# Depthwise convolution and channel rotation: the convolution's bands made by GpSimd from a mask and taps, without loading or turning them

## The chip, the cores and the metric

The kernel runs on one core of a Trainium2 chip. Its time is device microseconds; three runs of the kernel before took 558.16, 558.51 and 558.95 us (median 558.51). One more execution was recorded by the profiler.

## The reference

`x` is 16 x 128 x 64 x 64 in f32 (image, channel, row, column). What is computed:

```python
# _gn: 32 groups of 4 channels, mean and variance over (4 channels, 64, 64) of one image
x = x + depthwise_conv5x5(_gn(x), kernel)      # one 5x5 kernel for each channel, 16 of its 25 places filled, padding 2
x = x + einsum('hvc,bchw->bvhw', R, _gn(x))    # for each row h a 128x128 matrix over channels
```

The 16 places hold taps 1 to 8 of the channel's 3x3 weight, eight with a plus and eight with a minus sign. `R` is an input of 64 x 128 x 128.

## The kernel before

**First stage**, 32 groups of four channels. A group's `x` lies in a tile of `xin` (7 tiles): partition = image half n (0, 1) times 64 rows, free = 8 images x 4 channels x 64 columns. The convolution is a sum over five column offsets d: a band matrix of 64 x 64 over the rows (made of one column of taps) times the normalised tile shifted by d. Four such 64 x 64 products (two channels, two image halves) run in the four quarters of PE; two channels are one *pair* (`convolve(k, pair)`, L423), 40 matmuls in the trace, each pair in two banks of PSUM.

The steps are software pipelined by `for s in STEPS`, s from -3 to 34, in the same order on every engine. In step s:
- VectorE (DVE): the scale and shift of round s + 1 (`affine`, L373, L375), the add `x + conv` of group s - 1's second pair (L365), the statistics of that sum (L382), the statistics of `x` of group s + 3 (L389), three small operations for `spread` of round s + 2 (L398 to L403), the add of group s's first pair.
- TensorE (PE): the variance matmul of round s + 1 (L444, waits for `spread`), the first pair of group s, the mean matmul of round s + 2 (L454), the second pair.
- ScalarE (ACT): the square root (L314), evictions of PSUM to `y` (L305), `turn_taps` of group s + 1 (L294), two of eight images normalised into `padded` (L322), evictions.
- GpSimd (POOL): six of the eight images normalised (L267), after `affine` of that group.
- SyncE (SP): issues all DMAs: x of group s + 5 (L165, eight of 128 KB, 256 bytes a packet), the tap windows of group s + 2 (L172), the sum of group s - 1 to DRAM (L179, two of 512 KB).

The bands come through DRAM: DVE writes each channel's taps into a line of 400 numbers (L358), the lines are stored, and L172 reads for each of 64 partitions a window that starts one number later, 330 KB a group. Read like this the band is mirrored, so `turn_taps` copies it backwards, in two halves. A round's second half of `affine` holds the scales of the second normalisation; they are stored every eight groups (L186) and read back in another layout (L239).

**Second stage**, 32 *granules* of four rows and eight images, 1 MB each. `load_granule` (L223) reads into one of six tiles `tin`, ScalarE normalises five images (L335) and GpSimd three (L279), PE multiplies by the turned rotation (L482, rotations turned by L468, evicted by L343), DVE adds (L414), `store_granule` (L231) writes. The tiles of both stages share one area.

## Time and profile before

| what | us |
|---|---|
| median of three runs | 558.51 |
| the profiled execution, its own time | 558.65 |
| its span, first to last instruction | 556.8 |
| busy: PE, ScalarE, DVE, GpSimd | 450.6, 361.4, 347.2, 186.0 |
| PE convolution matmuls (L434), 2560 | 297.8 |
| granted TensorE clock, mean | 0.961 |

Read it as two stages, one up to about 370 us and one from there; shares over the whole span mix both. The times of an engine's queue (SPq) are the times in which it issues a DMA, not in which the DMA runs. A matmul's recorded length overlaps that of its neighbours, since four run at once.

### The profile page before, as it was taken

To read this page: it belongs to the slowest core of one execution; us is meant where nothing else is said; L and a number is where in the kernel's file an instruction comes from. 1 tells how busy PE (TensorE), PEld (TensorE's weight loads), DVE (VectorE), ACT (ScalarE), POOL (GpSimd) and SP (SyncE) were. 2 spreads that over 40 slices of the span, in tenths; PEclk is the share of its full clock that TensorE was granted. 3 is DMA by queue.
4 is the path that set the end of the run, shared out by engine and by line. 5 is a ranking of instruction groups with operands and counts; after the bars stand their busy time and mean duration, and the time that the engine had idled before them with its cause. 6 is when DMAs were issued, how large, how long until landed. Compare 5 with 4: busy or idle time off the path is not lost.

```text
span 556.8 us, 8400 instructions
## 1 busy us (share of the span) xinstructions
PE 450.6 (81%) x3024; PEld 172.8 (31%) x3024; DVE 347.2 (62%) x649; ACT 361.4 (65%) x598; POOL 186.0 (33%) x299
## 2 busy tenths in 40 slices
PE   0169999999898898989899899962998778788772
PEld 0123333333333333333333233321443333333330
DVE  3426787877876876686778768561574544544533
ACT  1066887787777678768877888842675455455550
POOL 0223534433533533353344335301343233233230
PEclk9999999999999999899899999995899998998997
DMA  6898788989889888889988989937999999999999
GB/s 155 200 201 167 204 218 222 244 220 226 244 216 226 225 225 216 219 216 235 223 224 243 226 224 308 274 85 235 375 394 397 394 396 397 396 398 396 395 394 325
DMA packets 214329, 150.03 MB, mean 269 GB/s; under 512 B 138384, under 2 KB 179472, under 8 KB 214288
## 3 DMA queue, kind: packets, MB, share of 16 engines
q1 hardware_dynamic: 214288, 149.49, 92.0%
q8 instruction: 24, 0.39, 0.3%
q14 instruction: 17, 0.14, 0.1%
HBM read 82.14 MB, written 67.33 MB: 268 GB/s over the span
## 4 chain that ended last, share of the span: by engine, by line
SPq 30%; DMA 28%; DVE 13%; ACT 12%; PE 11%; issue 4%; DVEq 0%
SPq L165 23%; DMA out_dram<-area 21%; ACT area L305 8%; PE ps L434 7%; DMA area<-tap_lines 7%; DVE stats L382 3%; DVE area L365 3%; DVE area L414 3%; DVE stats L389 3%; SPq L179 2%; PE ps L482 2%; ACT area L294 2%; SPq L227 2%; ACT area L322 2%; SPq L172 1%
## 5 line engine op out<-in xcount | busy, mean ns | idle before, releaser
L434 PE MATMUL ps<-area 64*64 64x512 f32 x2560 | 297.8, 607 | 8.5 <-ACT area L322 8.5
L267 POOL TENSOR_SCALAR area<-area,affine 128x256 f32<-128x256 f32 x192 | 132.9, 707 | 222.1 <-DVE affine L375 222.1
L305 ACT ACTIVATE area<-ps 64x512 f32<-64x512 f32 x256 | 150.4, 587 | 10.6 <-PE ps L434 5.9
L482 PE MATMUL ps<-area 128*128 128x512 f32 x256 | 123.7, 630 | 34.9 <-ACT area L343 28.1
L434 PEld LDWEIGHTS ps<-area 64*64 64x64 f32 x2560 | 93.2, 134 | 158.5 <-issue 156.9
L414 DVE TENSOR_TENSOR area<-ps,area 128x512 f32<-128x512 f32 x128 | 81.2, 685 | 85.7 <-DMA out_dram<-area 68.6
L335 ACT ACTIVATE area<-area,norm 128x256 f32<-128x256 f32 x160 | 82.1, 588 | 72.2 <-DMA area<-x_scratch 58.5
L365 DVE TENSOR_TENSOR area<-area 128x1024 f32<-128x1024 f32 x64 | 78.8, 1232 | 77.1 <-ACT area L305 77.0
L294 ACT ACTIVATE area<-area 64x1280 f32<-64x1280 f32 x64 | 81.3, 1270 | 60.1 <-DMA area<-tap_lines 59.2
L279 POOL TENSOR_SCALAR area<-area,norm 128x256 f32<-128x256 f32 x96 | 52.0, 555 | 132.9 <-DMA area<-x_scratch 81.0
L389 DVE BATCH_NORM_STATS2 stats<-area 128x6 f32<-128x512 f32 x128 | 79.9, 685 | 10.8 <-DMA area<-in_x_dram 10.8
L382 DVE BATCH_NORM_STATS2 stats<-area 128x6 f32<-128x512 f32 x128 | 80.7, 693 | 1.1
L482 PEld LDWEIGHTS ps<-area 128*128 128x128 f32 x256 | 48.7, 199 | 99.4 <-issue 40.5
L444 PE MATMUL ps<-spread,half_mean 128*128 128x16 f32 (+1 forms) x72 | 15.0, 283 | 36.3 <-DVE spread L403 35.6
L322 ACT ACTIVATE area<-area,affine 128x256 f32<-128x256 f32 x64 | 35.0, 594 | 0.8
L314 ACT ACTIVATE std<-ps,eps 128x16 f32<-128x16 f32 (+1 forms) x36 | 9.8, 271 | 36.7 <-PE ps L444 36.0
L444 PEld LDWEIGHTS ps<-spread,half_mean 128*128 128x128 f32 x72 | 11.5, 201 | 64.5 <-DVE spread L403 60.4
L454 PE MATMUL ps<-stats,half_mean 128*128 128x16 f32 (+1 forms) x72 | 14.7, 279 | 15.1 <-DVE stats L389 12.4
L454 PEld LDWEIGHTS ps<-stats,half_mean 128*128 128x128 f32 x72 | 11.3, 198 | 41.2 <-issue 41.2
L373 DVE RECIPROCAL affine<-std 128x16 f32<-128x16 f32 (+1 forms) x36 | 8.5, 236 | 14.9 <-ACT std L314 14.9
L468 PEld LDWEIGHTS ps<-ident,rot_all 128*128 128x128 f32 x64 | 8.2, 146 | 9.2 <-issue 9.2
L468 PE MATMUL ps<-ident,rot_all 128*128 128x128 f32 x64 | 10.1, 282 | 1.0 <-DVE affine L375 1.0
(22 smaller groups left out, 38.3 us busy)
## 6 DMA issues: line engine op xcount, KB each, us to landing
area<-in_x_dram SPq DMA_DIRECT2D x256, 128.0 KB, 3.3
x_scratch<-area SPq DMA_DIRECT2D x64, 512.0 KB, 6.0
area<-x_scratch SPq DMA_DIRECT2D x32, 1024.0 KB, 12.4
out_dram<-area SPq DMA_DIRECT2D x32, 1024.0 KB, 11.3
area<-tap_lines SPq DMA_DIRECT2D x32, 330.0 KB, 5.1
tap_lines<-line SPq DMA_DIRECT2D x1, 200.0 KB, 3.1
norm_scratch<-affine SPq DMA_DIRECT2D x8, 2.0 KB
rot_all<-_L_conv_rota_matrix_dram SPq DMA_DIRECT2D x4, 0.5 KB, 10.4
```

The lines of the kernel that those rows point to most:

```text
L165: sp.dma_start(xin[slot][n * HALF:(n + 1) * HALF, :, c], x[n * J:(n + 1) * J, k * GC + c].rearrange("j h w -> h j w")).then_inc(x_landed[s ...
L267: last = nc.gpsimd.tensor_scalar(padded[k % GRING][:, :, j, PAD:PAD + W], xin[k % XRING][:, j], affine[:, k, 0, 0, j:j + 1], affine[:, k, ...
L279: last = nc.gpsimd.tensor_scalar(gn[n % NRING][:, :, j], tin[n % IRING][:, :, j], norm2[:, n % 2, 0, j:j + 1], norm2[:, n % 2, 1, j:j + 1] ...
L294: nc.scalar.activation(taps[k % 2][n * HALF:(n + 1) * HALF], taps_raw[k % 2][0:H, :, :, H - 1::-1], ACT.Identity).then_inc(taps_ready, 1)
L305: last = nc.scalar.activation(y[k % YRING][rows, 2 * pair + c], ps[half, bank + n].rearrange("p (j w) -> p j w", j=J), ACT.Identity)
L335: last = nc.scalar.activation(gn[n % NRING][:, :, j], tin[n % IRING][:, :, j], ACT.Identity, scale=norm2[:, n % 2, 0, j:j + 1], bias=norm2 ...
L365: nc.vector.tensor_tensor(part, part, xin[k % XRING][:, :, cs].rearrange("p j c w -> p c j w"), ALU.add).then_inc(x1_ready, 1)
L382: last = nc.vector.bn_stats(out=stats[:, (s + 3) % 2, 1, 2 * q:2 * q + 2].rearrange("p j f -> p (j f)"), in_=y[(s - 1) % YRING][:, :, 2 * ...
L389: last = nc.vector.bn_stats(out=stats[:, k % 2, 0, 2 * q:2 * q + 2].rearrange("p j f -> p (j f)"), in_=xin[k % XRING][:, 2 * q:2 * q + 2]. ...
L414: nc.vector.tensor_tensor(tout[n % ORING][:, :, h], ps[:, (n * RH + h) % 6, :].rearrange("p (j w) -> p j w", j=J), tin[n % IRING][:, h], A ...
L434: last = nc.tensor.matmul(ps[half, bank + n], taps[k % 2][rows, 2 * pair + c, d], padded[k % GRING][rows, 2 * pair + c, :, d:d + W], start ...
L482: nc.tensor.matmul(ps[:, m % 6, :], rot_t[u % 2][:, h], gn[n % NRING][:, h], start=True, stop=True).then_inc(rotated, 1)
```

## The change

DVE now writes the 25 places of each channel's kernel (`line` is 25 numbers wide), the rows of the kernel in backward order. They are stored twice, one copy behind the other, and loaded so that partition m of a half holds the five rows rotated by m modulo 5 (`row_taps`, [128, 5, 640]): from place b modulo 5 it reads the tap that partition m needs for output row b. A mask (1 where |m - b| <= 2) is made once. For each group GpSimd multiplies the mask (repeated for 20 channel-and-column pairs) by `row_taps` (repeated for 13 blocks of five rows): one instruction with 1300 results a partition, into one of three `taps` tiles, two groups ahead. The second input is read in steps of 640 elements. The tap windows, their loads and `turn_taps` are gone. GpSimd normalises four images and ScalarE four.

The weight's load, the loads of `row_taps` (20 in all, the first ten for the first four groups) and the norms' stores and load are issued by ScalarE. On DVE the three operations for `spread` stand ahead of the x statistics. The rotation matrices are loaded from step 24 on instead of step 26. After the last store of the first sum, SyncE issues five loads of 112 channels (groups 0 to 27), once the four waits on older stores are met, then waits for all stores, loads the other 16 channels of the five granules, and goes on with whole granules; `tin` has seven tiles.

```diff
+TRING = 3
...
-POOL_J = 6
+POOL_J = 4
...
-IRING = 6
+IRING = 7
+EARLY = 5
+EARLY_SLOTS = (4, 5, 6, 0, 1, 2, 3)
+EARLY_GROUPS = 28
...
+ROT_STEP = GROUPS - 8
...
-    tap_lines = nc.dram_tensor("tap_lines", (C, LINE), F32, kind="Internal").ap()
+    tap_rows = nc.dram_tensor("tap_rows", (2 * TAPS, C, KW), F32, kind="Internal").ap()
...
-        line = sb("line", [C, LINE])
+        line = sb("line", [C, TAPS * KW])
+        near = sb("near", [P, HALF + BAND])
+        mask = sb("mask", [P, BAND])
+        row_taps = sb("row_taps", [P, TAPS, CK])
...
+        def granule_landings(n):
+            return 16 * (n // IRING + 1) + (16 if n % IRING < EARLY else 0)
...
-            def load_taps(k):
-                window = bass.AP(tensor=tap_lines.tensor, offset=k * GC * LINE,
-                                 ap=[[1, H], [LINE, GC], [1, WINDOW]])
-                sp.dma_start(taps_raw[k % 2][0:H].rearrange("p c d h -> p c (d h)"), window
-                             ).then_inc(taps_landed[k % 2], 16)
...
-            for k in range(2):
-                load(k)
-            sp.wait_ge(line_ready, len(POS_IDX + NEG_IDX))
-            sp.dma_start(tap_lines, line[:]).then_inc(line_stored, 16)
-            load(2)
-            load(3)
-            sp.wait_ge(line_stored, 16)
-            load_taps(0)
-            load_taps(1)
-            for k in range(4, XRING - 1):
+            for k in range(XRING - 1):
                 load(k)
...
-                if group(s + 2):
-                    sp.wait_ge(taps_ready, 2 * (s + 1))
-                    load_taps(s + 2)
                 if group(s - 1):
                     sp.wait_ge(x1_ready, 2 * s)
                     store(s - 1)
...
-                if s in range(GROUPS - 6, GROUPS - 6 + ROT_LOADS):
-                    n = s - (GROUPS - 6)
+                if s in range(ROT_STEP, ROT_STEP + ROT_LOADS):
+                    n = s - ROT_STEP
                     rows = slice(n * (H // ROT_LOADS), (n + 1) * (H // ROT_LOADS))
                     sp.dma_start(rot_all[:, rows], rota_src[:, rows]).then_inc(rot_landed, 16)
...
+            def load_granule(n, channels):
                 u, half = n // 2, n % 2
...
+                return sp.dma_start(tin[n % IRING][channels].rearrange("p h j w -> p h (j w)"),
+                                    x1_dram[channels, u * RH:(u + 1) * RH, half * J:(half + 1) * J, :].rearrange(
+                                        "c h j w -> c h (j w)"))
+
+            early, late = slice(0, EARLY_GROUPS * GC), slice(EARLY_GROUPS * GC, C)
+            for k in range(YRING):
+                sp.wait_ge(x1_stored[k], 32 * (EARLY_GROUPS // YRING))
+            for n in range(EARLY):
+                sp.wait_ge(x1_ready, 2 * (XRING * ((GROUPS - 1 - EARLY_SLOTS[n]) // XRING) + EARLY_SLOTS[n] + 1))
+                load_granule(n, early).then_inc(in_landed[n], 16)
+            for k in range(YRING):
+                sp.wait_ge(x1_stored[k], 32 * (GROUPS // YRING))
+            for n in range(EARLY):
+                load_granule(n, late).then_inc(in_landed[n], 16)
...
-            load_granule(0)
-            sp.wait_ge(norm2_stored, 32 * (GROUPS // NBATCH))
-            sp.dma_start(norm2[:], norm2_dram).then_inc(norm2_landed, 16)
-            for n in range(1, IRING):
-                load_granule(n)
+            for n in range(EARLY, IRING):
+                load_granule(n, slice(0, C)).then_inc(in_landed[n], 16)
...
                 if n + IRING < GRANULES:
-                    load_granule(n + IRING)
+                    load_granule(n + IRING, slice(0, C)).then_inc(in_landed[(n + IRING) % IRING], 16)
...
+            nc.gpsimd.memset(near[:], 0.0).then_inc(near_ready, 1)
+            for d in range(TAPS):
+                pool.wait_ge(near_ready, d + 1)
+                nc.gpsimd.affine_select(out=near[:], in_=near[:], compare_op=ALU.not_equal, fill=1.0, base=d - PAD,
+                                        pattern=[[-1, HALF + BAND]], channel_multiplier=1).then_inc(near_ready, 1)
+            pool.wait_ge(mask_ready, 2)
+
+            def spread_taps(k):
+                pool.wait_ge(taps_landed[0 if k < FIRST else 1], 16 * 2 * TAPS)
+                if k >= TRING:
+                    pool.wait_ge(convolved, 2 * (k - TRING + 1))
+                of_rows = mask[:].rearrange("p (b r) -> p b r", r=TAPS)
+                of_taps = row_taps[:, :, k * GCK:(k + 1) * GCK].rearrange("p r c -> p c r")
+                nc.gpsimd.tensor_tensor(
+                    taps[k % TRING].rearrange("p c (b r) -> p c b r", r=TAPS),
+                    bass.AP(tensor=of_rows.tensor, offset=of_rows.offset, ap=[of_rows.ap[0], [0, GCK], *of_rows.ap[1:]]),
+                    bass.AP(tensor=of_taps.tensor, offset=of_taps.offset,
+                            ap=[*of_taps.ap[:2], [0, BLOCKS], of_taps.ap[2]]),
+                    ALU.mult).then_inc(taps_ready, 1)
+
             for s in STEPS:
+                if group(s + 2):
+                    spread_taps(s + 2)
                 k = s + 1
...
-
-            def turn_taps(k):
-                act.wait_ge(taps_landed[k % 2], 16 * (k // 2 + 1))
-                if k >= 2:
-                    act.wait_ge(convolved, 2 * (k - 1))
+            act.wait_ge(line_ready, len(POS_IDX + NEG_IDX))
+            for n in range(2):
+                act.dma_start(tap_rows[n * TAPS:(n + 1) * TAPS].rearrange("r c k -> c r k"),
+                              line[:].rearrange("c (r k) -> c r k", r=TAPS)).then_inc(line_stored, 16)
+            act.wait_ge(line_stored, 32)
+            for part, cols in enumerate((slice(0, FIRST * GCK), slice(FIRST * GCK, CK))):
                 for n in range(2):
-                    nc.scalar.activation(taps[k % 2][n * HALF:(n + 1) * HALF],
-                                         taps_raw[k % 2][0:H, :, :, H - 1::-1], ACT.Identity).then_inc(taps_ready, 1)
+                    for row in range(TAPS):
+                        first = (PAD - row) % TAPS
+                        rows = row_taps[n * HALF + row:(n + 1) * HALF:TAPS, :, cols]
+                        source = tap_rows.rearrange("r c k -> r (c k)")[first:first + TAPS, cols]
+                        act.dma_start(rows, bass.AP(tensor=source.tensor, offset=source.offset,
+                                                    ap=[[0, (HALF - row + TAPS - 1) // TAPS], *source.ap])
+                                      ).then_inc(taps_landed[part], 16)
...
-                    turn_taps(k)
...
+                if group(s - 3) and (s - 2) % NBATCH == 0:
+                    store_norms(s - 2 - NBATCH)
+
+            act.wait_ge(norm2_stored, 32 * (GROUPS // NBATCH))
+            act.dma_start(norm2[:], norm2_dram).then_inc(norm2_landed, 16)
...
-                act.wait_ge(in_landed[n % IRING], 16 * (n // IRING + 1))
+                act.wait_ge(in_landed[n % IRING], granule_landings(n))
...
-                    at = (place % KW) * PITCH + MID + place // KW - PAD
+                    at = (TAPS - 1 - place // KW) * KW + place % KW
...
+            dve.wait_ge(near_ready, TAPS + 1)
+            for n in range(2):
+                nc.vector.tensor_scalar(mask[n * HALF:(n + 1) * HALF], near[n * HALF:(n + 1) * HALF, n * HALF:n * HALF + BAND],
+                                        1.0, None, ALU.mult).then_inc(mask_ready, 1)
...
-                if group(s + 3):
-                    k = s + 3
-                    dve.wait_ge(x_landed[k % XRING], 16 * 2 * GC * (k // XRING + 1))
-                    for q in range(J // 2):
-                        last = nc.vector.bn_stats(
-                            out=stats[:, k % 2, 0, 2 * q:2 * q + 2].rearrange("p j f -> p (j f)"),
-                            in_=xin[k % XRING][:, 2 * q:2 * q + 2].rearrange("p j c w -> p (c w) j"))
-                if is_round(s + 3):
-                    last.then_inc(stats_ready, 1)
                 if is_round(s + 2):
                     r = s + 2
                     k = norms(r)
...
+                if group(s + 3):
+                    k = s + 3
+                    dve.wait_ge(x_landed[k % XRING], 16 * 2 * GC * (k // XRING + 1))
+                    for q in range(J // 2):
+                        last = nc.vector.bn_stats(
+                            out=stats[:, k % 2, 0, 2 * q:2 * q + 2].rearrange("p j f -> p (j f)"),
+                            in_=xin[k % XRING][:, 2 * q:2 * q + 2].rearrange("p j c w -> p (c w) j"))
+                if is_round(s + 3):
+                    last.then_inc(stats_ready, 1)
                 if group(s):
                     add(s, 0)
...
-                    pe.wait_ge(taps_ready, 2 * (k + 1))
+                    pe.wait_ge(taps_ready, k + 1)
...
-                        last = nc.tensor.matmul(ps[half, bank + n], taps[k % 2][rows, 2 * pair + c, d],
+                        last = nc.tensor.matmul(ps[half, bank + n], taps[k % TRING][rows, (2 * pair + c) * KW + d, 0:H],
```

The orders show what stands where. First GpSimd, from the end of its set-up to the third group's normalisation, before; `area` holds `xin`, `padded`, `y` and `taps`.

```order
L257 AFFINE_SELECT ident<-ident 128x128
L267 TENSOR_SCALAR area<-area,affine 128x4x64 [waits affine_ready]
L267 TENSOR_SCALAR area<-area,affine 128x4x64 x5
L267 TENSOR_SCALAR area<-area,affine 128x4x64 [waits affine_ready]
L267 TENSOR_SCALAR area<-area,affine 128x4x64 x5
L267 TENSOR_SCALAR area<-area,affine 128x4x64 [waits convolved,affine_ready]
```

The same place after; L262 is the product, L278 the normalisation.

```order
L246 AFFINE_SELECT ident<-ident 128x128
L249 MEMSET near 128x129
L252 AFFINE_SELECT near<-near 128x129 [waits near_ready] x5
L262 TENSOR_TENSOR area<-mask,row_taps 128x1300 [waits taps_landed0,mask_ready]
L262 TENSOR_TENSOR area<-mask,row_taps 128x1300 [waits taps_landed0]
L278 TENSOR_SCALAR area<-area,affine 128x4x64 [waits affine_ready]
L278 TENSOR_SCALAR area<-area,affine 128x4x64 x3
L262 TENSOR_TENSOR area<-mask,row_taps 128x1300 [waits taps_landed0]
L278 TENSOR_SCALAR area<-area,affine 128x4x64 [waits affine_ready]
L278 TENSOR_SCALAR area<-area,affine 128x4x64 x3
L262 TENSOR_TENSOR area<-mask,row_taps 128x1300 [waits convolved,taps_landed0]
```

Two products precede the first normalisation, and from then on one precedes each; from the fourth on it waits for the convolution that read the tile's last contents.

Next DVE, one step in the middle of the first stage, before; `dev` and `spread` are the small operations, `128x1024` is an add of one pair.

```order
L365 TENSOR_TENSOR area<-area 128x1024 [waits y_ready]
L382 BN_STATS stats<-area 128x6 [waits x1_ready]
L382 BN_STATS stats<-area 128x6 x3
L389 BN_STATS stats<-area 128x6 [waits x_landed6]
L389 BN_STATS stats<-area 128x6 x3
L398 TENSOR_TENSOR dev<-stats,ps 128x16 [waits mean_ready]
L401 TENSOR_TENSOR dev<-dev 128x16 [waits dev_ready]
L403 SCALAR_TENSOR_TENSOR spread<-stats,dev 128x16 [waits dev2_ready]
L365 TENSOR_TENSOR area<-area 128x1024 [waits y_ready]
```

The same step after (L400 is the add, L417 and L436 the two statistics).

```order
L400 TENSOR_TENSOR area<-area 128x1024 [waits y_ready]
L417 BN_STATS stats<-area 128x6 [waits x1_ready]
L417 BN_STATS stats<-area 128x6 x3
L424 TENSOR_TENSOR dev<-stats,ps 128x16 [waits mean_ready]
L427 TENSOR_TENSOR dev<-dev 128x16 [waits dev_ready]
L429 SCALAR_TENSOR_TENSOR spread<-stats,dev 128x16 [waits dev2_ready]
L436 BN_STATS stats<-area 128x6 [waits x_landed6]
L436 BN_STATS stats<-area 128x6 x3
L400 TENSOR_TENSOR area<-area 128x1024 [waits y_ready]
```

The statistics of x moved behind `spread`, everything else kept its place.

## Rows read from the trace of the kernel before

**Rows 1.** Table of stretches: length, busy time and instructions by engine, clock, DMA.
```profile
60.00:100.00 40.00, 39.54 (x345) 14.10 (x348) 33.01 (x62) 33.45 (x53) 17.56 (x26) 1.00 0.85 223
120.00:340.00 220.00, 200.37 (x1712) 71.00 (x1704) 166.49 (x307) 171.38 (x265) 84.70 (x122) 0.98 0.89 228
...
440.00:460.00 20.00, 14.54 (x39) 6.18 (x38) 9.19 (x15) 10.90 (x22) 6.25 (x12) 1.00 1.07 396
```
**Rows 2.** Timeline of PE, late first stage: start, length, engine, line, operation.
```profile
345.70 0.39 PE L454 MATMUL ps<-stats,half_mean 128*128 128x16 f32 x2
...
355.32 0.39 PE L454 MATMUL ps<-stats,half_mean 128*128 128x8 f32 x2
```
**Rows 3.** Timeline of the start, in brackets idle before and releaser.
```profile
2.47 1.06 DVE L358 TENSOR_SCALAR line<-w_sb 128x1 f32<-128x1 f32 x16 [0.58 <-DMA w_sb<-in_L_conv_weight_dram]
...
28.83 2.56 ACT L294 ACTIVATE area<-area 64x1280 f32<-64x1280 f32 x2 [10.21 <-DMA area<-tap_lines]
...
32.66 7.47 PE L434 MATMUL ps<-area 64*64 64x512 f32 x40 [7.87 <-ACT area L322]
```
**Rows 4.** Timeline between the stages.
```profile
365.25 4.55 PE L434 MATMUL ps<-area 64*64 64x512 f32 x40
...
372.78 1.23 DVE L365 TENSOR_TENSOR area<-area 128x1024 f32<-128x1024 f32 x1 [1.92 <-ACT area L305]
...
381.91 0.40 SPq L227 DMA_DIRECT2D area<-x_scratch  x1
...
387.16 2.56 ACT L335 ACTIVATE area<-area,norm 128x256 f32<-128x256 f32 x5 [6.50 <-DMA norm<-norm_scratch]
...
396.37 0.38 SPq L234 DMA_DIRECT2D out_dram<-area  x1
```
**Rows 5.** Chain of waits in order of time, one lap: start, length, what.
```profile
203.17 1.25 DVE area L365
...
211.89 4.36 DMA area<-tap_lines
...
217.57 1.27 ACT area L294
...
224.94 1.25 DVE area L365
```
**Rows 6.** Waits, whole span: us in total, times, longest.
```profile
PEld ps L444 <- DVE spread L403: 60.4, 31, 5.8
ACT area L294 <- DMA area<-tap_lines: 59.2, 25, 10.2
```
**Rows 7.** Timeline of SyncE's queue, 60 to 120 us.
```profile
62.22 8.77 SPq L165 DMA_DIRECT2D area<-in_x_dram  x8
71.03 0.63 SPq L172 DMA_DIRECT2D area<-tap_lines  x1
...
83.75 9.38 SPq L165 DMA_DIRECT2D area<-in_x_dram  x8
```
**Rows 8.** The x loads' issues and landing; the tap line's store.
```profile
L165 SPq DMA_DIRECT2D area<-in_x_dram x256: 596/636/2357, 1.2 to 319.7; - x128
...
DMA to landing us min/median/max: 2.7/3.3/6.5
...
tap_lines<-line SPq DMA_DIRECT2D x1, 200.0 KB, 3.1
```
**Rows 9.** GpSimd and DVE by line (ns min/median/max), and GpSimd's timeline.
```profile
L267 POOL TENSOR_SCALAR area<-area,affine x192: 547/556/1628, 19.2 to 356.3; 128x256 f32<-128x256 f32 x192
...
L365 DVE TENSOR_TENSOR area<-area x64: 1218/1226/1411, 42.7 to 372.8; 128x1024 f32<-128x1024 f32 x64
...
1.54 0.29 POOL L257 TENSOR_SCALAR_AFFINE_SELECT ident<-ident 128x128 f32<-128x128 f32 x1 [0.24 <-POOL ident L255]
...
202.24 4.20 POOL L267 TENSOR_SCALAR area<-area,affine 128x256 f32<-128x256 f32 x6 [7.18 <-DVE affine L375]
```

More of the change, by code:

```diff
@@ L21 @@
 WP = W + 2 * PAD
-PITCH = H + 2
-MID = H - 1
-WINDOW = KW * PITCH
-LINE = 400
+BLOCKS = (H + TAPS - 1) // TAPS
+BAND = BLOCKS * TAPS
+CK = C * KW
+GCK = GC * KW
+FIRST = 4
 POS_IDX = (0, 2, 4, 10, 14, 20, 22, 24)
@@ L60, in sem @@
             return ctx.enter_context(nc.semaphore(name))
-        area = sb("area", [P, 36 * 1024])
+        area = sb("area", [P, 31 * 1024])
         used = [0]
@@ L77, in conv_rotate_kernel @@
         y = [piece((GC, J, W)) for _ in range(YRING)]
-        taps_raw = [piece((GC, KW, PITCH)) for _ in range(2)]
-        taps = [piece((GC, KW, H)) for _ in range(2)]
+        taps = [piece((GCK, BAND)) for _ in range(TRING)]
         used[0] = 0
-        tin = [piece((RH, J, W)) for _ in range(IRING)]
+        slots = [piece((RH, J, W)) for _ in range(IRING)]
+        tin = [slots[n] for n in EARLY_SLOTS]
         tout = [piece((J, RH, W)) for _ in range(ORING)]
@@ L112, in conv_rotate_kernel @@
         x_landed = [sem(f"x_landed{n}") for n in range(XRING)]
+        near_ready = sem("near_ready")
+        mask_ready = sem("mask_ready")
         taps_landed = [sem(f"taps_landed{n}") for n in range(2)]
@@ L158, in _ @@
         def _(sp):
-            sp.dma_start(w_sb[:], weight.rearrange("c o a b -> c (o a b)")).then_inc(w_landed, 16)
             def load(k):
```

27 lines of the change are left out of this document (9 added, 18 removed).

## The prediction

> **What bounds the kernel now.** I read five views in this order.
>
> First the page's slices and the table of stretches: there are two stages. In [rows 1] the second one (from 400 us on) moves 396 GB/s at a DMA share of 1.07, and no engine is busy for more than four fifths of it. That is transfers at their limit: 64 transfers of 1 MB (32 in, 32 out), 1.0486 MB / 396 GB/s = 2.65 us each, 169.5 us in all. The first stage is different: DMA share 0.85 to 0.89, PE busy 99% from 60 to 100 us and 91% from 120 to 340 us.
>
> Second, what PE could do. Near the end of the first stage it runs without a gap: in [rows 2] the statistics matmuls of one kind stand at 345.70 and 355.32, one group of four channels in 9.62 us. From the start of the first convolution, 32.66 [rows 3], to the end of the last, 365.25 + 4.55 = 369.80 [rows 4], 337.1 us pass for 32 groups, 10.54 each. So 0.92 us a group is lost on average.
>
> Third, the chain of waits says what to. In [rows 5] one lap goes from an add of DVE (203.17) through eight issues of x loads in SyncE's queue, then one load of the tap windows (211.89), which takes 4.36 us to land, ScalarE's turn of them, its two normalised images, four evictions, and the next add (224.94): 21.77 us for two groups, 10.9 each. The lap exists because each group's tap load is issued behind the next x loads and is needed one group later. ScalarE's waits agree: 59.2 us for the tap windows [rows 6].
>
> Fourth, the start [rows 3]: ScalarE has waited 10.21 us for the taps when it turns the first ones at 28.83, and PE begins at 32.66. Fifth, the end of the stage [rows 4]: the last convolution ends at 369.80, the last add at 374.0, SyncE starts the first load of the rotation at 381.91, the norms land at 387.16 and the first output leaves at 396.37.
>
> **Start of the first stage.** Removed: the tap windows' trip and the turning. Added: one weight load, two small stores and twenty small loads, all issued by ScalarE, and two products on POOL ahead of the first normalisation. The line of taps is finished at about 3.6 us (its 16 writes start at 2.47 and take 1.06 [rows 3]). An issue costs 0.38 to 0.40 us for the loads and stores of the rotation [rows 4] and 0.63 for a tap window [rows 7]. Two stores issued by about 4.9, landed about 3.1 us later as the tap line does now [rows 8], say 8.5. Ten loads of the first part: issued 12.5 to 15, landed 14.5 to 18.3; I take 17.3. Then two products of 3.7 us (below) and four normalisations of 0.547 us [rows 9] on POOL, 9.6 us: PE begins at 27.0 (24.2 to 28.0). ScalarE, after all twenty issues, is free at 16.5 to 21.5 us, before POOL is done, so its delay of the first square root is covered. Gain 5.7 us.
>
> **A group in the first stage.** ScalarE loses two turns of 1.27 us [rows 5] and gains two images of at most 0.6 us each (the length of an eviction's instruction), so it has over 1 us a group less to do. SyncE loses one issue. The transfers lose 330 KB of the 2.4 MB a group. DVE's work stays, but the three small operations that make `spread` come before the x statistics instead of behind them, 2.5 us earlier; the variance matmul of PE waits for them, 60.4 us in all [rows 6]. So DVE is no longer late unless something holds its adds.
>
> POOL is the engine to watch. Of its six images four stay: 4 x 0.547 = 2.19 us. New is one product of 128 x 1300 with two inputs, one of them read in steps of 640 elements. No row shows such an instruction. The nearest: a normalisation of 256 elements takes 0.547 us, a select of 128 elements 0.29 us [rows 9]. Their difference is 2.0 ns an element, so 1300 elements with one input would be 0.29 + 1172 x 0.0020 = 2.6 us: the lower bound. With every element read twice the slope doubles: 5.0 us; three times it, for the steps, is 7.3 us, the upper bound. I take 3.7 us, between the first two and nearer to the row. The Trainium skill, GPSIMD Engine Reference, section 3 (elementwise accounting), gives 4497 ns for a two-input tensor_tensor of 2048 elements, by which ours would be an estimated 2.9 us; its section 7 adds half for steps over 8 bytes.
>
> Where does the product stand? In the order it follows the normalisation of the group before and waits for the end of the convolution one group back, so it starts with PE's new group, at t = 0. PE's group needs, at t = 9.62, POOL's images and DVE's spread. POOL alone: 3.7 + four images 2.2 + the stretch that an add gives it. That stretch is in [rows 9]: one normalisation lasted up to 1.628 us where the median is 0.556, and six take 4.20 us with an add of DVE inside (203.17, [rows 5]) where six times 0.547 is 3.28, so about 1.0 us. Sum 6.9 to 7.9, done before 9.62. The adds are not stretched in turn: 1.218 to 1.411 us [rows 9].
>
> A rule speaks against this. The row shows POOL giving way while short POOL instructions run. The Trainium skill, SBUF — State Buffer, section "Who interferes with whom", says that a DVE instruction with two SBUF inputs and a GpSimd one that reads SBUF take the shared port whole: whoever is second waits to the other's end. Here DVE's add of the finished pair asks at about t = 2.9 (ScalarE's square root and four evictions of 0.6 us come first), in the middle of the product. If DVE gives way, the add runs from 3.7 instead: add 1.23, y statistics about 2.5, the three small operations 0.6, with gaps an end at t = 8.2, and the variance matmul wants it at 9.3. It fits either way, until the product exceeds 4.8 us. From there each us of it costs 1 us a group, 32 us in all.
>
> So PE sets the group: 9.62, of which I add 0.03 for small slips, 32 x 9.65 = 308.8, plus 2.9 for the first forty matmuls, which ran at 7.47 instead of 4.56 us [rows 3, 4]: 311.7 us against 337.1. Gain 25.4 us. What could be late next is SyncE: between 62.22 and 83.75 it issued without rest, 10.8 us a group [rows 7]. Without the tap issue of 0.68 us (with its gap) that is 10.1, or 9.9 if the bytes count (0.33 MB at 396 GB/s is 0.83 us), still above 9.62. But x is loaded six groups ahead and first read three groups ahead, while the tap window was loaded one group ahead of its use; the debt of 26 groups x 0.3 to 0.5 us = 8 to 13 us fits the two groups (19 us) of lead. I cost it at nothing; if the lead is not there, 12 us.
>
> **Between the stages.** SyncE no longer waits for the norms: after the last store it issues five early loads of 112 channels (4.6 MB), then five of the last 16 channels, then two whole ones. From the last convolution's end (T): issue at T + 5.5; store's rest 2.65, early loads 11.6, so T + 19.8. The late pieces are 128 KB each. At the full rate 0.33 us, but they touch 16 partitions only; the nearest row in size, x loads, are issued in 0.64 us each (median), 0.68 with the gap, and the quickest takes 2.7 us to land [rows 8]. I take 0.7 (3.5 us for five), ends 0.33 and 2.7. The first granule is whole at T + 22.5, behind the norms (T + 17.4 now). The first output leaves 9.2 us after (387.16 to 396.37 [rows 4]), T + 31.7, where it is T + 26.6 now. In its place more is loaded: seven granules instead of six. Remaining 57 transfers x 2.65 = 151.0, and an end of 2.7 (half of what the span now has beyond 12.1 + 169.5): T + 185.4 against 556.8 - 369.8 = 187.0. Gain 1.6 us only. The Trainium skill, SBUF — State Buffer, "Door 1: The DMA port swizzle", has 16 partitions reach few of the 16 ports; by it a late piece would be an estimated 1.2 us, 2.5 us more for five. No row shows a transfer to so few partitions.
>
> **Sum.** 27.0 + 311.7 + 185.4 = 524.1 us span, plus the 1.85 us between the span and the profiled run's time (558.65 - 556.8): 526.0. The profiled run is 0.14 us above the median of 558.51, which I ignore.
>
> **Rivals.**
> - A, the transfers of the first stage stay the bound. For: SyncE's unbroken issue [rows 7]. Against: the DMA share of 0.85 to 0.89 where 1.07 is full, and the longer lead of x. Price 26 x 0.45 = 12 us: 538.
> - B, POOL's product is 5.5 us and DVE waits for it. For: two inputs, wide steps. Against: the add's rows. 0.7 us a group x 32 = 22: 548.
> - C, slower than before: the product is POOL's whole group. At 7.5 us POOL needs 7.5 + 1.07 + 2.19 + 0.2 = 10.96 us a group, 32 x 1.31 = 42 more: 568; with DVE held too, about 610. The 32.7 us gained are gone at 10.67 us a group: from a product of 5.8 us (DVE held) or 7.2 us (POOL alone). For: nothing shows the price. Against: it takes about three times the slope of the row.
> - D, the late pieces cost 2.7 us each and nothing is gained between the stages: 10 us more, 536.
>
> **Numbers.** My forecast 0.56 (518 to 536 by the bounds above), A 0.12, D 0.06, B 0.10, C 0.13, all else 0.03, of it 0.02 for no change (within 0.2%, 1.1 us, about what a measurement of this kernel tells from nothing). Faster 0.56 + 0.12 + 0.06 + 0.10 + 0.01 = 0.85. The range goes from 514 (start, late pieces and POOL all at their good ends, and some us more) to 552, past B; C is left out.
>
> **What would show it.** The product's mean: 3.7 us, under 4.8. Groups at 9.62 to 9.7 us by the mean matmuls, no idle of PE on spread or POOL. First convolution at 27. ScalarE's waits on taps gone, SyncE resting on DVE's adds for at least part of a group. After the last convolution, an output store at about +32, and then 396 GB/s. I am wrong if PE idles for POOL (C), the add waits for ScalarE no longer but for POOL (B), or SyncE still issues without rest while DVE waits for x (A).

## The result and the profile after

| | before | changed |
|---|---|---|
| median | 558.73 us (4 runs) | 565.87 us (4 runs) |
| span | 556.8 | 564.3 |
| first convolution starts | 32.7 | 33.1 |
| first stage, to the end of the last convolution | 337.1 | 327.3 |
| from there to the end of the span | 187.0 | 203.9 |

The ratio is 1.0122, interval 1.0102 to 1.0142: 1.2% slower, where 526 was forecast. The lower rows are from the profiled execution. By the terms of the sum, the start is 6.1 us later than forecast (33.1 for 27.0), the first stage 15.6 longer (327.3 for 311.7) and the rest 18.5 longer (203.9 for 185.4).

**A group in the first stage.** The page after, costliest groups: busy time, mean ns, idle before.

```profile
L262 POOL TENSOR_TENSOR area<-mask,row_taps 128x1300 f32<-128x1300 f32 x32 | 116.1, 3628 | 82.0 <-PE ps L469 62.5
L400 DVE TENSOR_TENSOR area<-area 128x1024 f32<-128x1024 f32 x64 | 140.1, 2189 | 8.0 <-ACT area L331 7.9
```

The product takes 3.63 us, as forecast. The add (L365 before, median 1.226 us [rows 9]) now takes 2.19 on average. Timeline of one group of the changed kernel:

```profile
207.62 3.63 POOL L262 TENSOR_TENSOR area<-mask,row_taps 128x1300 f32<-128x1300 f32 x1 [2.00 <-PE ps L469]
207.69 4.55 PE L469 MATMUL ps<-area 64*64 64x512 f32 x40
...
208.98 3.35 DVE L400 TENSOR_TENSOR area<-area 128x1024 f32<-128x1024 f32 x1
...
212.53 0.17 DVE L410 SCALAR_TENSOR_TENSOR affine<-ps,affine 128x16 f32<-128x16 f32 x1
212.62 1.22 DVE L400 TENSOR_TENSOR area<-area 128x1024 f32<-128x1024 f32 x1
...
212.85 0.37 PE L489 MATMUL ps<-stats,half_mean 128*128 128x16 f32 x2 [0.61 <-DVE affine L410]
213.14 4.55 PE L469 MATMUL ps<-area 64*64 64x512 f32 x40
...
217.88 3.64 POOL L262 TENSOR_TENSOR area<-mask,row_taps 128x1300 f32<-128x1300 f32 x1 [2.00 <-PE ps L469]
```

The product ends at 211.25 and the add that began at 208.98 (it is the first pair's) ends 1.08 us later. Behind it in DVE's queue stands `affine`; PE's mean matmul waits for that and idles 0.61 us; the second pair follows; its end lets the next product start. That is a lap: 3.63 for the product, 1.08 to the add's end, 0.5 to the mean matmul, 0.3, 4.55 for the second pair and 0.2 to the next product, 10.26 us, the distance of the two products. The lap of SyncE's taps [rows 5] is gone, and this one is in its place. 0.64 us above PE's 9.62 [rows 2], over 27 groups, is 17 us.

**The start**, chain of waits in order of time, changed kernel:

```profile
4.07 8.48 DMA tap_rows<-line
...
14.03 0.82 ACTq L311
...
20.76 2.77 DMA row_taps<-tap_rows
...
23.68 7.12 POOL area L262 x2
30.81 2.19 POOL area L278 x4
```

The small store (640 pieces of 20 bytes a copy) takes 8.5 us to land, where 3.6 was forecast, and an issue 0.8 us (forecast 0.4 to 0.65). Whether the pieces or the x loads beside them cost the store its time, no run separates. The kernel before turned its first taps at 28.83 [rows 3]; here GpSimd's first normalisation stands at 30.81. ScalarE would have held it as long: its twenty issues end at 29.9, its first square root follows at 29.96 and DVE's `affine` at 30.50.

**Between the stages**: length, busy times by engine, clock, DMA share, GB/s in stretches of the changed kernel (the early loads to 112 partitions; then the late ones to 16).

```profile
378.00:386.00 8.00, 0.00 (x0) 0.00 (x0) 0.00 (x0) 0.00 (x0) 0.00 (x0) 0.50 1.07 233
390.00:394.00 4.00, 0.00 (x0) 0.00 (x0) 0.00 (x0) 0.00 (x0) 0.00 (x0) 0.50 1.10 125
```

And its timeline, beside [rows 4]:

```profile
396.60 2.56 ACT L365 ACTIVATE area<-area,norm 128x256 f32<-128x256 f32 x5 [25.38 <-DMA area<-x_scratch]
...
406.65 0.38 SPq L226 DMA_DIRECT2D out_dram<-area  x1
```

The DMA engines are as busy as at 396 GB/s (share 1.07, [rows 1]) and move 233, so five early loads of 0.92 MB take 19.7 us. The first output leaves 46.3 us after the last convolution; it was 26.6.

### The profile page after: what moved, and what is told of

The parts are those of the page before. It is cut to its first block, busy times and chain, and to the rows that moved or that the text cites. A ratio compares the mean times of both kernels' runs of the same rounds, so it can differ in the third digit from the quotient of the medians.

```text
span 564.3 us, 8377 instructions
## 1 busy us (share of the span) xinstructions
PE 442.3 (78%) x3024; PEld 169.1 (30%) x3024; DVE 405.1 (72%) x651; ACT 312.0 (55%) x598; POOL 266.6 (47%) x273
## 4 chain that ended last, share of the span: by engine, by line
DVE 52%; DMA 20%; PE 11%; SPq 10%; POOL 2%; ACTq 1%; ACT 1%; issue 1%; DVEq 0%; POOLq 0%
DVE area L400 22%; DMA out_dram<-area 14%; DVE stats L417 13%; DVE stats L436 12%; SPq L208 8%; PE ps L469 6%; DMA area<-x_scratch 4%; PE ps L517 4%; DMA tap_rows<-line 2%; ACTq L311 1%; SPq L226 1%; POOL area L262 1%; DVE area L449 1%; DVE dev L427 1%; DVE spread L429 1%
## 5 line engine op out<-in xcount | busy, mean ns | idle before, releaser
L469 PE MATMUL ps<-area 64*64 64x512 f32 x2560 | 292.9, 598 | 0.3 <-POOL area L278 0.3
L517 PE MATMUL ps<-area 128*128 128x512 f32 x256 | 122.3, 619 | 54.3 <-DVE area L449 27.6
L262 POOL TENSOR_TENSOR area<-mask,row_taps 128x1300 f32<-128x1300 f32 x32 | 116.1, 3628 | 82.0 <-PE ps L469 62.5
L400 DVE TENSOR_TENSOR area<-area 128x1024 f32<-128x1024 f32 x64 | 140.1, 2189 | 8.0 <-ACT area L331 7.9
L469 PEld LDWEIGHTS ps<-area 64*64 64x64 f32 x2560 | 91.4, 132 | 147.2 <-issue 145.5
L365 ACT ACTIVATE area<-area,norm 128x256 f32<-128x256 f32 x160 | 82.1, 588 | 86.8 <-PE ps L517 54.8
L278 POOL TENSOR_SCALAR area<-area,affine 128x256 f32<-128x256 f32 x128 | 95.8, 763 | 46.7 <-DVE affine L410 46.7
L347 ACT ACTIVATE area<-area,affine 128x256 f32<-128x256 f32 x128 | 66.5, 591 | 68.1 <-DVE affine L410 68.0
L436 DVE BATCH_NORM_STATS2 stats<-area 128x6 f32<-128x512 f32 x128 | 80.4, 692 | 9.9 <-DMA area<-in_x_dram 9.9
L517 PEld LDWEIGHTS ps<-area 128*128 128x128 f32 x256 | 47.1, 195 | 118.3 <-DVE area L449 51.9
L417 DVE BATCH_NORM_STATS2 stats<-area 128x6 f32<-128x512 f32 x128 | 80.8, 696 | 1.1
L503 PE MATMUL ps<-ident,rot_all 128*128 128x128 f32 x64 | 10.1, 282 | 1.0 <-DVE affine L410 1.0
```

Of the source, the lines that this page charges most:

```text
L262: nc.gpsimd.tensor_tensor(taps[k % TRING].rearrange("p c (b r) -> p c b r", r=TAPS), bass.AP(tensor=of_rows.tensor, offset=of_rows.offset, ...
L278: last = nc.gpsimd.tensor_scalar(padded[k % GRING][:, :, j, PAD:PAD + W], xin[k % XRING][:, j], affine[:, k, 0, 0, j:j + 1], affine[:, k, ...
L347: last = nc.scalar.activation(padded[k % GRING][:, :, j, PAD:PAD + W], xin[k % XRING][:, j], ACT.Identity, scale=affine[:, k, 0, 0, j:j + ...
L365: last = nc.scalar.activation(gn[n % NRING][:, :, j], tin[n % IRING][:, :, j], ACT.Identity, scale=norm2[:, n % 2, 0, j:j + 1], bias=norm2 ...
L400: nc.vector.tensor_tensor(part, part, xin[k % XRING][:, :, cs].rearrange("p j c w -> p c j w"), ALU.add).then_inc(x1_ready, 1)
L417: last = nc.vector.bn_stats(out=stats[:, (s + 3) % 2, 1, 2 * q:2 * q + 2].rearrange("p j f -> p (j f)"), in_=y[(s - 1) % YRING][:, :, 2 * ...
```

## The experiments

Theory L: one engine's instruction holds the memory port until it is done, and DVE's add, which has two inputs there, waits for GpSimd's long one. Theory P: loads to 112 and 16 partitions are slow in themselves. Columns of the table: first convolution's start, first stage, rest, each from one profiled execution; "ratio" is to the kernel before; "one" stands for a kernel that ran once and has none. Three profiles with the start of the changed kernel left as it is (the kernel itself, full_granules, early_64_late_64) begin at 33.1, 31.8 and 31.7, so a start tells nothing below about 1.5 us.

| run | us | ratio (95%) | start | stage | rest |
|---|---|---|---|---|---|
| full_granules | 552.36 | 0.988 (0.984-0.992) | 31.8 | 328.1 | 188.7 |
| product_behind | 582.88 | 1.043 (1.039-1.047) | 31.3 | 345.7 | 204.2 |
| product_in_four | 549.36 | 0.984 (0.980-0.987) | 34.0 | 309.1 | 205.4 |
| three_mended | 566.17 | 1.013 (1.009-1.017) | 29.7 | 345.5 | 188.9 |
| four_whole_start | 533.51 | 0.956 (0.952-0.961) | 32.8 | 310.6 | 187.9 |
| four_whole_start_two_first | 532.45 | 0.955 (0.949-0.960) | 33.0 | 308.9 | 188.4 |
| one_input_product | 547.45, one | | 31.6 | 310.0 | 204.0 |
| early_64_late_64 | 561.14, one | | 31.7 | 328.7 | 199.0 |
| start_shared_too | 542.68 | 0.973 (0.969-0.978) | 27.3 | 323.8 | 188.4 |
| long_one_input | 560.38, one | | 32.6 | 323.0 | 203.0 |
| product_in_two | 547.85, one | | 32.9 | 309.8 | 203.3 |
| before_spread_early | 557.50 | 0.998 (0.996-1.001) | 32.2 | 334.3 | 187.6 |
| rotation_loads_late | 527.63 | 0.945 (0.938-0.952) | 27.0 | 311.0 | 189.1 |

**full_granules**: whole granules again, one load of 128 channels each behind all stores.

```diff
-            for n in range(EARLY):
...
-                load_granule(n, early).then_inc(in_landed[n], 16)
             for k in range(YRING):
                 sp.wait_ge(x1_stored[k], 32 * (GROUPS // YRING))
             for n in range(EARLY):
-                load_granule(n, late).then_inc(in_landed[n], 16)
+                load_granule(n, slice(0, C)).then_inc(in_landed[n], 16)
```

> The changed kernel with one thing undone: after the last convolution it waits for all stores of the first sum and then loads seven whole granules of 128 channels, instead of five of 112 channels and five of 16. Theory P (the loads to 112 and to 16 partitions are slow in themselves): from the end of the last convolution to the end of the span 203.9 us falls to 183 to 187, the first output store from +46.3 to about +27; time 546 to 550. Rival Q (the first stage's late stores or the norms' way over ScalarE's queue hold the second stage): stays above +40 for the first store, time 560 or more. The first stage stays at about 327 us under both.

The rest falls by 15.2 us, the first store (counted from the last convolution's end) from +46.3 to +31.2, the time to 552.36. The same kind of stretch as above, in this run:

```profile
378.00:382.00 4.00, 0.00 (x0) 0.00 (x0) 0.00 (x0) 0.00 (x0) 0.00 (x0) 0.50 1.07 388
```

388 GB/s at the share at which the changed kernel moved 233. The store's +27 was missed by 4 us, the rest's 187 and the time's 550 by about 2: seven whole loads lie ahead of the norms' small transfers, which landed at +22.2. Theory P holds, with that part of Q. Why 112 partitions are slow it doesn't show.

**product_behind**: the product after the normalisation.

```diff
-                if group(s + 2):
-                    spread_taps(s + 2)
                 k = s + 1
...
                     last.then_inc(normed_pool, 1)
+                if group(s + 2):
+                    spread_taps(s + 2)
```

> The changed kernel with GpSimd's product behind the normalisation of its step instead of ahead of it, all else the same. Theory L (DVE's add waits for the whole product when it starts inside it, and the add, the scales, the mean matmul, the second pair and the next product form a ring): the product now runs beside the statistics, which read one input; adds return to a mean near 1.25 us from 2.19, a group takes 9.62 to 9.75 us instead of 10.27, the first stage 310 to 315 us instead of 327; time 550 to 556. Rival M (the product loads GpSimd or memory as such, wherever it stands): adds or statistics stay stretched, a group stays above 10.1 us, time 563 or more.

Both theories as written failed. Adds are free again (mean 1.21 us), as L had it, but the kernel is slower; a group is longer than 10.1 us, as M had it, but no add and no statistics are stretched. The timeline shows why:

```profile
211.82 3.62 POOL L262 TENSOR_TENSOR area<-mask,row_taps 128x1300 f32<-128x1300 f32 x1
...
212.46 3.01 DVE L427 TENSOR_TENSOR dev<-dev 128x16 f32<-128x16 f32 x1
```

An operation on 16 numbers, 0.17 us otherwise, takes 3.01 us and ends 0.03 us after the product. It squares `dev`, so it too has two inputs in memory. It shows the lock more clearly than the add does, since its size plays no part. `spread`, which stands behind it, is late, PE waits 1.2 us for that, and a group takes 10.9 us.

**product_in_four** (and **product_in_two**): the same results in four or two instructions.

```diff
-                nc.gpsimd.tensor_tensor(
-                    taps[k % TRING].rearrange("p c (b r) -> p c b r", r=TAPS),
...
+                size = GCK // 4
+                for q in range(4):
+                    part = slice(q * size, (q + 1) * size)
...
+                    last = nc.gpsimd.tensor_tensor(
+                        taps[k % TRING][:, part].rearrange("p c (b r) -> p c b r", r=TAPS),
...
```

> The changed kernel with the product cut into four instructions of 5 column pairs (325 results each), same place, same results. Theory L (the add waits to the end of the instruction that it meets): an add waits 0.9 us at most, so the group's 10.27 us become about 9.7 to 9.9 and adds average 1.3 to 1.8 us; time 551 to 558. Rival M (the product takes the port for its whole length, in however many pieces): an add that falls into it is still stretched to 3.3 us, group 10.2 us or more, time 564 or more.

> The product in two instructions of 10 column pairs (650 results, about 1.85 us each). Theory L: the first pair's add, which comes 1.3 us after the product starts, waits for the first piece only, about 0.5 us; mean add about 1.5 us, group 9.62 to 9.75 us, first stage 309 to 313; span 548 to 552. If what matters is the sum of both pieces (they follow each other without letting DVE in), the group stays at 10.27 us and the span at 564.

```profile
208.38 0.40 PE L483 MATMUL ps<-spread,half_mean 128*128 128x16 f32 x2
208.63 6.03 POOL L265 TENSOR_TENSOR area<-mask,row_taps 128x325 f32<-128x325 f32 x4 [1.43 <-PE ps L473]
...
209.03 1.74 DVE L404 TENSOR_TENSOR area<-area 128x1024 f32<-128x1024 f32 x1
...
218.00 0.40 PE L483 MATMUL ps<-spread,half_mean 128*128 128x16 f32 x2
```

Four pieces: the add waits 0.5 us, goes between two pieces, GpSimd takes 6.03 us instead of 3.63 as it waits in turn, and nobody needs it earlier. The group takes 9.62 us: PE is the bound, the stage 309.1 (forecast of the prediction 311.7). Two pieces do as well (309.8), although adds average 1.91: the first pair's add, the one in the lap, takes 1.38 us, 0.15 more than alone. What counts is which operation waits.

The same run shows that short instructions with one input hold DVE too. The normalisations follow each other every 0.54 us here, and each small operation ends 0.02 to 0.03 us after one of them (those that began at 215.18 and 215.72):

```profile
214.64 1.64 POOL L282 TENSOR_SCALAR area<-area,affine 128x256 f32<-128x256 f32 x3
...
215.41 0.35 DVE L431 TENSOR_TENSOR dev<-dev 128x16 f32<-128x16 f32 x1
215.80 0.51 DVE L433 SCALAR_TENSOR_TENSOR spread<-stats,dev 128x16 f32<-128x16 f32 x1
```

**three_mended**: whole granules, product behind, second ten row-tap loads in SyncE's queue.

```diff
             for k in range(XRING - 1):
+                if k == 4:
+                    sp.wait_ge(line_stored, 32)
+                    load_row_taps(sp, 1, slice(FIRST * GCK, CK))
                 load(k)
```

> Three edits of the changed kernel at once: whole granules, product behind the normalisation, and the second ten loads of row taps issued by SyncE (behind the x of group 3) instead of ScalarE. If the three costs are apart from each other: first convolution at 27 to 30 us instead of 33.1, first stage 310 to 315, rest 183 to 187, span 521 to 530, time 523 to 532. If one mended part uncovers the transfers of the first stage as the bound (SyncE issued for 9.6 to 10.6 us a group without rest), the stage stays at 320 or more and the time at 535 or more.

The start came as expected (29.7), the rest as in full_granules (188.9, 2 us over what was expected); the stage carries product_behind's fault (345.5 beside 345.7). So the run says nothing on the transfers of the first stage.

**four_whole_start**: the same with the product in four at its old place; **four_whole_start_two_first**: besides, SyncE waits for the norms after two granules,

```diff
-            for n in range(EARLY):
+            for n in range(2):
                 load_granule(n, slice(0, C)).then_inc(in_landed[n], 16)
+            sp.wait_ge(norm2_landed, 16)
```

> The three edits that the runs so far support, at once: product in four pieces at its old place, seven whole granules, second ten row-tap loads issued by SyncE. If their costs add: first convolution at 29.7 us, first stage 309.1 (as with four pieces alone), rest 188.7 (as with whole granules alone), span 527.5, time 529. Rival (the transfers of the first stage become the bound once PE runs at 9.62 us a group from 29.7 on, with the row taps' 1.7 MB in SyncE's queue): first stage 313 us or more, time 533 or more.

> The same, and SyncE issues two granules, waits for the norms to have landed, and issues the other five then. With seven ahead the norms landed 22.2 us after the last convolution, 17.4 in the kernel before. Theory N (the norms' small store and load lie behind the granules' packets, and the second stage starts with them): norms at +17 to +18, first output store at +26.5 instead of +31.2; but the transfers rest for some us meanwhile, so the rest of the span is 184 to 188.7, time 525 to 529. Rival (what counts is bytes moved by then, the norms don't matter): rest 190 or more.

The stage and the rest add up (310.6 and 187.9); the start does not (32.8 for 29.7), since two products in pieces stand ahead of the first normalisation again and PE waits 10.1 us for GpSimd. With it the times of 529 and 525 to 529 were missed by 3 to 5 us.

With two granules first the norms land at +18.6 instead of +22.2, and the first store leaves at +27.9 instead of +31.2:

```profile
369.83 0.38 SPq L234 DMA_DIRECT2D out_dram<-area  x1
...
390.24 1.32 SPq L234 DMA_DIRECT2D out_dram<-area  x1
```

So theory N is right on what the second stage starts with. But nothing is gained by it: the fifth store leaves at +48.3, where it was +48.6, and the rest is 188.4 for 187.9 (N allowed 184 to 188.7). The transfers rest meanwhile, at a DMA share of 0.59 and 192 GB/s from 360 to 364 us.

**one_input_product** and **long_one_input**: does it take two inputs on GpSimd's side?

```diff
+                if k >= TRING:                       # long_one_input only
...
+                    nc.gpsimd.tensor_scalar(
+                        spare[:].rearrange("p (c b r) -> p c b r", b=BLOCKS, r=TAPS),
...
-                nc.gpsimd.tensor_tensor(
+                nc.gpsimd.tensor_scalar(
                     taps[k % TRING].rearrange("p c (b r) -> p c b r", r=TAPS),
...
-                    ALU.mult).then_inc(taps_ready, 1)
+                    0.1, 0.0, ALU.mult, ALU.add).then_inc(taps_ready, 1)
```

> The changed kernel with the product replaced by a one-input instruction of the same 1300 results (mask times 0.1; the taps are left out of the bands), same place, same waits. Theory L1 (DVE's two-input operations wait only for a GpSimd instruction with two inputs; those with one input give way, as the 0.55 us normalisations seemed to): the first pair's add keeps 1.22 us, a group takes 9.62 us. Theory L2 (any GpSimd instruction that reads holds the port to its end): the add is stretched to the end of the instruction, about 1 us if it takes 2.6 us, mean add 1.6 to 1.8 us; group 9.62 to 9.7.

> As the one-input run (the taps left out of the bands), with another one-input instruction of 3900 results ahead of it in the steps from group 3 on, into a spare tile. At the 1.28 us that 1300 results took alone it is 3.8 us long, as the product's 3.63, and stands in the same place. Theory L1 (only two-input GpSimd instructions make DVE's two-input operation wait): DVE's adds keep 1.22 us though they start inside it, GpSimd is stretched by them, a group takes 9.62 us. Theory L2 (the length is what counts, any instruction that reads): adds wait to its end, mean above 1.8 us, group above 10.0 us.

Both kernels leave the taps out of the bands. The short one seemed to speak for L1 (mean add 1.222, group 9.62), but its add began 0.2 us ahead of GpSimd's instruction, and it was GpSimd that waited: 1.28 us alone, 2.13 here.

```profile
206.95 1.21 DVE L398 TENSOR_TENSOR area<-area 128x1024 f32<-128x1024 f32 x1
207.16 2.13 POOL L262 TENSOR_SCALAR area<-mask 128x1300 f32<-128x1300 f32 x1 [4.17 <-PE ps L467]
```

The long one decides:

```profile
215.56 3.46 POOL L265 TENSOR_SCALAR spare<-mask 128x3900 f32<-128x3900 f32 x1 [1.28 <-issue]
...
217.62 2.47 DVE L406 TENSOR_TENSOR area<-area 128x1024 f32<-128x1024 f32 x1
```

The add ends at 220.09, 1.07 us after the instruction's end at 219.02. L1 falls: one input is enough, and the group takes 10.08 us. What counts is how much of GpSimd's instruction is left when the add comes.

**early_64_late_64**: `EARLY_GROUPS = 16`.

> The changed kernel with the early loads cut to 64 channels (groups 0 to 15) and the late ones raised to 64, same ten issues. In the changed kernel transfers to 112 partitions moved 233 GB/s and to 16 partitions 125 GB/s, at the same full DMA share, whole ones 396. Theory P1 (a transfer's rate goes by how evenly its partitions spread over the paths into the memory, 64 reach half): about 200 to 220 GB/s through both, 5.2 MB in 25 us, first output store at +40 to +46, span within 3 us of the changed kernel's. Theory P2 (only the small late ones are slow): 64 moves near 390 GB/s, first store at +31, span 549 or less.

```profile
378.00:386.00 8.00, 0.00 (x0) 0.00 (x0) 0.00 (x0) 0.00 (x0) 0.00 (x0) 0.50 1.07 210
```

210 GB/s here, 201 to 218 in every stretch of 4 us from 374 to 398, through both halves, and the first store at +41.4: P1, against P2's 390 and +31. P1 had the span within 3 us of the changed kernel's; it is 5.0 us shorter.

**before_spread_early**: only DVE's order, on the kernel before.

> The kernel before with one part of the change alone: DVE's three small operations stand ahead of the x statistics. The taps' lap sets its first stage, so by that theory nothing is gained over most of it: 0 to 3 us less, 555 to 559. If PE's wait for spread (60.4 us in the list of waits) was on the path, 5 us or more are gained: 553 or less.

No difference that the runs can tell, though the profiled stage is 2.8 us shorter. ScalarE still waits 63.3 us for taps.

**start_shared_too** and **rotation_loads_late**.

```diff
             for k in range(XRING - 1):
+                if k == 2:
+                    sp.wait_ge(line_stored, 32)
+                    load_row_taps(sp, 1, 0, slice(0, FIRST * GCK))     # the other five by ScalarE
+                if k == 4:
+                    for n in range(2):
+                        load_row_taps(sp, n, 1, slice(FIRST * GCK, CK))
                 load(k)
...
-                if group(s + 2):
+                if group(s + 2) and s != -1:                         # group 1: behind the first normalisation
                     spread_taps(s + 2)
...
-ROT_STEP = GROUPS - 8
+ROT_STEP = GROUPS - 5                                                # rotation_loads_late only
```

> The version with four pieces, whole granules and two granules ahead of the norms, plus the start: the first ten row-tap loads shared by ScalarE and SyncE (five each, SyncE behind the x of group 1), and GpSimd makes the product of group 1 behind the first normalisation. In the version before it, PE idled 10.1 us at the start for GpSimd, whose products of groups 0 and 1 took from about 22.5 to 30.5. Expected: row taps landed at about 19 to 20 us instead of 23, first convolution at 26 to 28 us instead of 33.0, stage 309 to 311, rest 188.4; time 525 to 528. Rival (the small tap lines' store, 8.5 us, and x of group 2, now later, hold it): 530 or more.

> As the version with the start shared, with the four loads of the rotation matrices in steps 27 to 30, behind the last x load (step 26), instead of 24 to 27. Debt theory: SyncE's lap of 9.9 to 10.6 us against PE's 9.62 has used up the lead of x by step 24, and 4 MB of rotation matrices between the last x loads turn it into a wait; without them DVE waits for x 0 to 3 us in all, stage 309 to 312, first convolution still at 27.3, rest 188 to 190, time 526 to 529. Rival (the x of group 2, or the lead itself, is too short by then): the long groups stay, 536 us or more.

The start came as expected (27.3), the time did not (525 to 528 expected): groups of 9.62 us up to the 27th and 9.67 for the 28th, then 16.65 and 16.26.

```profile
288.89 1.62 SPq L219 DMA_DIRECT2D rot_all<-_L_conv_rota_matrix_dram  x1
...
304.36 1.57 SPq L219 DMA_DIRECT2D rot_all<-_L_conv_rota_matrix_dram  x1
304.99 2.49 DVE L444 BATCH_NORM_STATS2 stats<-area 128x6 f32<-128x512 f32 x4 [6.37 <-DMA area<-in_x_dram]
```

From 30 us on DVE waits 15.6 us for x. Of that 1.09 us end at 289.35, and the load waited for was issued by 287.1, ahead of the first rotation load: the lead was used up before these came. With the rotation loads behind the last x load it is 5.8 us (0 to 3 expected), the long groups are gone (the longest is 10.68), and the version takes 527.63 us, the fastest. The debt theory holds, in two parts: SyncE's laps of about 10 us use up the lead, and the rotation loads then turn it into long waits.

## Why the prediction was wrong

The 40.2 us between the forecast span and the measured one lie in all three terms: 6.1 in the start, 15.6 in the first stage, 18.5 in the rest.

- **The product, 3.7 us**: right (3.63, never over 3.64).
- **"It fits either way, until the product exceeds 4.8 us"**: the step that failed in the first stage. "Done before 9.62" held for GpSimd itself, whose images end 8.3 us after the product's start. But I followed DVE only as far as `spread`, from the second pair's add at t = 2.9. Carried on by the same numbers, 8.2 plus 2.5 us of x statistics is t = 10.7, which is t = 1.1 of the next group: there the first pair's add asks, 1.4 us into the next product in the trace, and `affine`, on which PE's second pair depends, is queued behind it. Rival B had the mechanism but at a product of 5.5 us; with the right add the bound is an estimated 3.0 us (10.26 - 9.62 = 0.64 less than 3.63). Four runs carry this: the product in four and in two gives 9.62 us, the one-input instruction of nearly the same length (3.46) 10.08, and behind the normalisation it holds another operation. Cutting the product in four is worth 16.5 us of time by itself (549.36 for 565.87).
- **"The row shows POOL giving way while short POOL instructions run"**: misread. These rows of the kernel before have the same lock:

```profile
202.78 0.56 POOL L267 TENSOR_SCALAR area<-area,affine 128x256 f32<-128x256 f32 x1
203.17 1.23 DVE L365 TENSOR_TENSOR area<-area 128x1024 f32<-128x1024 f32 x1 [1.03 <-ACT area L305]
...
203.31 1.52 POOL L267 TENSOR_SCALAR area<-area,affine 128x256 f32<-128x256 f32 x1
```

The add comes 0.17 us before a normalisation's end and ends 1.07 us after it, as it does behind the long product; the next normalisation waits for the add. With so little left to wait for the add's length hides it. The longest add, 1.41 us, came at 47.92 with 0.34 us left and ended 1.07 us after.

- **The rule of the Trainium skill** (SBUF — State Buffer, "Who interferes with whom": whoever is second waits to the other's end) agrees with every one of the rows shown, those of the kernel before too. I weighed it at the wrong add.
- **PE as the bound at 9.62 us a group, stage 311.7**: right once the lock is out of the way (308.9 to 311.0 in six runs).
- **Start, 27.0**: mechanism right, sizes off: the tap store 8.5 us for 3.6, the issues 0.8. ScalarE's twenty issues ended at 29.9, which I had put at 21.5 at most; that they were covered by GpSimd's work came true by 0.1 us only. 27.0 was reached by sharing the issues and moving group 1's product behind the first normalisation.
- **The rest, "early loads 11.6"**: the step that failed between the stages, a mis-sized term and the largest single one. 4.6 MB at 396 GB/s; the trace has 233, so 19.7 us. I doubted only the late pieces, whose 0.66 MB took about 5 us (forecast 3.5), and put rival D there. The granule was whole at +36.2 us, not +22.5, and the first store left 14.6 us later than forecast. The other 3.9 us lie behind it: the remaining 57 transfers and the end took 157.6 us, which I had put at 153.7 (151.0 and 2.7). Whole granules are worth 13.5 us of time by themselves (552.36).
- **SyncE's debt costed at nothing**: right for the changed kernel, since its groups of 10.26 us hide it. It is the next bound: with PE at 9.62 from 27.3 us on, the lead was used up by the 28th group. The 12.8 us between the stages of start_shared_too and rotation_loads_late are near rival A's 12 by luck: most of it is the rotation loads, which rival A doesn't have; without them the debt leaves about 2 us (311.0 beside 308.9).

What stays open: why loads to 112 partitions move 233 GB/s, and what makes the small tap store take 7.0 to 8.5 us.

## What to carry to other kernels

When an engine's order is followed to a deadline, follow it once round to where it meets itself; the operation that waits need not be the one in view. Lengths that hardly vary don't show that nobody waits: look at what was running when the operation came, and how long after its end the operation ended. A long GpSimd instruction beside a DVE operation with two inputs in memory was cheap in pieces and dear in one, also where the DVE operation is tiny. Splitting a load by channels so that it can start early cost more here than the start gave, since the pieces were not 128 partitions wide.

## What the hardware showed

- DVE's operations with two inputs in memory ended 1.07 to 1.08 us (adds of 128 x 1024) or 0.02 to 0.03 us (128 x 16) after the GpSimd instruction that they met, whether it took 3.6 or 0.56 us and had one input or two. With pieces of 1.0 us the add waited 0.5 us. Where the add came first, GpSimd waited: 2.13 us for 1.28, 1.52 for 0.56. In the kernel before an add that came at 106.92, 0.05 us after a normalisation's recorded start, still went first (1.23 us, the normalisation 1.62).
- On GpSimd 1300 results took 3.63 us with two inputs, one in steps of 640 elements, and 1.28 us with one input (shortest of 32).
- At a DMA share of 1.07 to 1.10 loads moved 388 GB/s to 128 partitions, 233 to 112, 210 to 64 and 125 to 16. The Trainium skill (SBUF — State Buffer, "Door 1: The DMA port swizzle") has a rate for 64 partitions as for 32, half of the full one: the 210 agree; for 112 the section's table has no row.
